# Five shifted sums packed without a gap, and two ScalarE copies of 400 elements in place of four of 200

## What is computed

```python
x = x + _L0_conv_ref(_gn(x), ...)   # sign, grouped 3x3 convolutions, batch norms
x = x + _L1_conv_ref(_gn(x), ...)   # deformable 3x3 attention over 8 groups
```

```python
off = om[..., :2 * K].reshape(n, h, w, G, K, 2) * OFFSET_SCALE
mask = om[..., 2 * K:]
...
sampled = gather(y0i, x0i, (1 - ty) * (1 - tx)) + gather(y0i, x0i + 1, (1 - ty) * tx) \
    + gather(y0i + 1, x0i, ty * (1 - tx)) + gather(y0i + 1, x0i + 1, ty * tx)
out = jnp.einsum('nhwgk,nhwgkc->nhwgc', mask, sampled)
out = out.reshape(n, L, c) @ op_w.T
```

## Time and profile before

| what | value |
| --- | --- |
| median of three runs | 2926.51 us |
| the profiled execution | 2924.83 us |
| its span, from the first instruction to the last | 2923.0 us |
| busy: TensorE, ScalarE, VectorE, GpSimd | 2430.8, 2259.7, 2205.6, 1917.6 us |
| `windows`, one pass (L1258) | 310 ns, x4032 |
| `copy_weights`, one copy (L1135) | 605 ns, x896 |
| `copy_om` (L960) | 1063 ns, x224 |

### The profile page before, as it was taken

The page is one execution under the profiler, slowest core; times in us unless marked ns, Lnnn a source line. Parts: engine busy times, 40 slices in busy tenths (PEclk is TensorE's granted clock), DMA queues, the critical chain, the costliest instruction groups (busy, mean ns, idle before and its releaser), DMA issues. The chain is left out here.

```text
span 2923.0 us, 100581 instructions
## 1 busy us (share of the span) xinstructions
PE 2430.8 (83%) x40456; PEld 2021.2 (69%) x40456; DVE 2205.6 (75%) x3095; ACT 2259.7 (77%) x4721; POOL 1917.6 (66%) x1452
## 2 busy tenths in 40 slices
PE   3999779993688888888888888888888888888887
PEld 2666556772577777777777777777777777777786
DVE  3555423334989897989888898989898988989773
ACT  2444256662989889898989898898989898989892
POOL 1000000003888888888988888888988898988892
PEclk8999889996899999999999999999999999999998
DMA  4555579975577677777777777777778777877675
GB/s 103 130 132 144 143 182 265 263 199 172 124 191 203 181 195 192 188 191 190 204 194 192 187 200 195 197 183 193 199 189 198 188 196 187 206 179 190 177 176 147
DMA packets 356164, 538.18 MB, mean 184 GB/s; under 512 B 171728, under 2 KB 258256, under 8 KB 355536
## 3 DMA queue, kind: packets, MB, share of 16 engines
q1 hardware_dynamic: 296656, 422.71, 60.3%
q10 hardware_dynamic: 59136, 110.11, 10.8%
HBM read 312.82 MB, written 219.77 MB: 182 GB/s over the span
## 5 line engine op out<-in xcount | busy, mean ns | idle before, releaser
L1109 ACT ACTIVATE dwt<-xp,wts 128x224 f32<-128x224 f32 x2016 | 797.3, 484 | 40.8 <-ACT wst L1135 31.8
L1280 PE MATMUL acc_p<-abuf,vbd 128*32 128x136 f32 (+5 forms) x20480 | 710.4, 291 | 54.9 <-issue 46.0
L1280 PEld LDWEIGHTS acc_p<-abuf,vbd 128*32 128x32 f32 (+1 forms) x20480 | 645.9, 145 | 117.7 <-issue 60.5
L979 DVE TENSOR_TENSOR pr<-mh_p,ht 128x864 f32<-128x864 f32 x672 | 668.9, 1051 | 23.2
L1258 PE MATMUL win_p<-pr,smat 128*128 128x160 f32 x4032 | 626.7, 310 | 27.3 <-POOL pr L1065 15.8
L246 PE MATMUL cv<-cin,wb 128*64 128x392 bf16 x6912 | 590.4, 333 | 25.8 <-ACT cin L225 25.8
L1258 PEld LDWEIGHTS win_p<-pr,smat 128*128 128x128 f32 x4032 | 570.4, 194 | 51.2 <-issue 22.4
L246 PEld LDWEIGHTS cv<-cin,wb 128*64 128x64 bf16 x6912 | 401.4, 110 | 208.7 <-ACT cin L225 25.9
L1048 POOL TENSOR_TENSOR dwt<-dwt 128x896 f32<-128x896 f32 x224 | 516.3, 2305 | 4.7 <-ACT dwt L1109 4.7
L1062 POOL TENSOR_TENSOR pr<-pr 128x576 f32<-128x576 f32 x224 | 317.3, 1417 | 187.8 <-DVE pr L979 187.8
L1135 ACT ACTIVATE wst<-win_p 128x200 f32<-128x200 f32 x896 | 388.6, 605 | 62.4 <-PE win_p L1258 38.7
(11 more groups left out here) (132 smaller groups left out, 2674.9 us busy)
## 6 DMA issues: line engine op xcount, KB each, us to landing
abuf<-weight_scratch SPq DMA_DIRECT2D x1568, 96.0 KB, 3.3
weight_scratch<-wst ACTq DMA_DIRECT2D x112, 960.0 KB, 6.2
xt<-x SPq DMA_DIRECT2D x128, 392.0 KB, 7.6
rows_scratch<-vsb SPq DMA_DIRECT2D x224, 128.0 KB, 2.1
vbd<-rows_scratch SPq DMA_DIRECT2D x896, 32.0 KB, 3.2
x_scratch<-xt SPq DMA_DIRECT2D x64, 392.0 KB, 6.6
y<-x SPq DMA_DIRECT2D x64, 392.0 KB, 4.4
x3h<-x_scratch SPq DMA_DIRECT2D x64, 392.0 KB, 4.9
```

Of the source, the lines that this page charges most:

```text
L979: dve.tensor_tensor(pr[:, j % 2, slots, :, :, :].rearrange("p k e x z -> p e k (x z)"), mh[:, a, :, :].rearrange("p (k x) z -> p k (x z)", ...
L1109: ins = act.activation(dwt[:, j % 2, k, :].rearrange("p (r w) -> p r w", w=W), image[:, r:r + BR, k % 3:k % 3 + W], ACT.Identity, scale=dw ...
L1280: mm = pe.matmul(acc_p[32 * (2 * s + b):32 * (2 * s + b) + 32, 0:2 * TN].rearrange("p (t w r) -> p t w r", t=BR, r=2)[:, t0:t1 + 1, x0:x1, :],
```

## The change

In PSUM, the five sums of `win_p` lay 172 columns apart, with gaps, in the order (shift, row, half b, pixel k, group). Now they follow each other at 160 columns, and within a row's 32 columns the order is group, then pixel. The order of the 32 is set where `oms` is made: `copy_om` now reads, for each of the 216 numbers of a row, the four rows' numbers, 256 elements apart in PSUM, and writes them side by side; before it read runs of four groups. `hats`, `mask_hats`, `products` and `merge` work element by element and are the same.

At 160 columns the fourth sum (e = 3) begins at column 480 and would cross the end of a PSUM bank at 512. So each of its two terms is computed in two matmuls, of 32 and of 128 columns.

`copy_weights` then needs two copies in place of four: for r = 0 and 1 it takes the two pixels of that parity. One copy goes over 4 groups x 50 (sums and half rows) x 2 pixels = 400 elements, and the cells of `wst` that it fills are the same as before. Before, neighbouring elements of a copy went to cells 480 elements apart (one group to the next); now pairs of them go to cells two elements apart.

```diff
-WP = 172
...
                     dve.tensor_tensor(
-                        oms[:, j % 2, :, :].rearrange("q w (b k g) -> q (w b) k g", b=2, g=GS),
-                        om_p[:, :].rearrange("q (k z) -> q k z", k=BR)[:, :, 0:OMC].rearrange("q k (v g) -> q v k g", g=GS),
-                        ombt[:, :].rearrange("q (v g) -> q v g", g=GS).unsqueeze(2).broadcast_to([LANES, 6 * TAPS, BR, GS]),
+                        oms[:, j % 2, :, :].rearrange("q w (g k) -> q (w g) k", k=BR),
+                        om_p[:, :].rearrange("q (k z) -> q z k", k=BR)[:, 0:OMC, :],
+                        ombt[:, :].unsqueeze(2).broadcast_to([LANES, OMC, BR]),
                         ALU.add).then_inc(om_ok, 1)
...
-                    for k in range(BR):
-                        to = 2 * BR * (2 - 2 * (k % 2)) + BR * u + k
+                    for r in range(2):
+                        to = 4 * BR * (1 - r) + BR * u + r
                         cells = wst[:, 0, to:to + 1]
                         ins = act.activation(
-                            bass.AP(cells.tensor, cells.offset, [cells.ap[0], [PC, CT], [2 * BR, 2 * RT], [BAND, GS]]),
-                            win_p[:, 0:CT * WP].rearrange("p (e z) -> p e z", e=CT)[:, :, 0:RT * BR * G].rearrange(
-                                "p e (m k g) -> p e m k g", k=BR, g=GS)[:, :, :, k, :],
+                            bass.AP(cells.tensor, cells.offset, [cells.ap[0], [PC, GS * CT], [2 * BR, 2 * RT], [2, 2]]),
+                            win_p[:, 0:CT * RT * BR * G].rearrange("p (m g k r) -> p r g m k", g=GS, k=2, r=2)[:, r],
                             ACT.Copy)
...
-                        to = WP * e
+                        cuts = (0, 1, RT) if e == 3 else (0, RT)
                         for n, (a, b) in enumerate(terms):
-                            mm = pe.matmul(win_p[:, to:to + 160], smat[:, e, :],
-                                           pr[:, j % 2, 0:RT, a, b, :],
-                                           start=n == 0, stop=n == len(terms) - 1)
+                            for m0, m1 in zip(cuts, cuts[1:]):
+                                mm = pe.matmul(win_p[:, BR * G * (RT * e + m0):BR * G * (RT * e + m1)], smat[:, e, :],
+                                               pr[:, j % 2, m0:m1, a, b, :],
+                                               start=n == 0, stop=n == len(terms) - 1)
```

## The result

The changed kernel takes 2937.93 us (median of 17 executions; the kernel before, in the same session, 2927.75, median of 18). An eighteenth execution of the changed kernel, slow at 4013.00 us with a granted clock of 0.557 where the others have 0.944 to 0.955, is left out. The ratio is 1.0034, 95% interval 1.0024 to 1.0044: slower by 0.34%, some 10 us, where the prediction said 4 us less. The time lies inside the stated range of 2905 to 2947 us, on the wrong side of the kernel before. The profiled execution took 2944.45 us (span 2942.7), 19.6 more than that of before, so the profile shows the effect somewhat too large.

What follows compares the result with a forecast made beforehand. With four engines nearly level, waits named the bound: GpSimd in some tiles, VectorE in those with next-image sums. Terms -5 + 3 - 2 + 0 = -4 us gave a 2922.5 us median; 8-in-10 range 2905 to 2947.

Steps and rivals of the forecast that it cites:

- What bounds the kernel: Loop over 224 tiles: four engines nearly level, so waits name the bound; hardly anybody waits for ScalarE.
- ScalarE's copies: Weight copies out of PSUM: 0.7 us less per tile, credited as -5 us, half of what others waited for ScalarE.
- TensorE's shifted sums (+3): The cut fourth sum's added matmuls: 0.3 us more per tile, mostly covered by waits, counted as +3 us.
- TensorE's clock (-2): Longer windows shorten TensorE's idle gaps before `misc`; a tenth fewer drops to half clock, -2 us.
- `oms` (0): VectorE's copy `oms`, now reading PSUM in steps of 1 KB: no longer than before, 0 us.
- The second: Rival: VectorE's `oms` pays for its strided PSUM read; 3024 us, or 2943 at half the price; chance 0.11.
- the fourth: Rival: ScalarE sets the pace after all, so all 157 us come back, 2770 us; chance 0.02.
- The third: Rival: TensorE becomes the bound between the sums, its work per tile passing GpSimd's 8.55 us; 2954 us; chance 0.07.
- The first: Rival: TensorE's and ScalarE's lateness is worth more: 8 us of half clock, 11 of waiting; 2910 us; chance 0.23.
- the signs for "wrong": `oms` above 1.4 us; VectorE's `misc` waits up over 20 us with TensorE's wait gone; or span falling with ScalarE's busy time.

Runs made afterwards that it cites:

- e1: Changed kernel with the sums starting at column 32, so no term is cut; new order and two copies stay: ratio to the kernel before 1.0032.
- e4: As e1 (new order, no cut), but with four copies of 200 elements in place of two of 400: ratio to the kernel before 1.0007.
- e2: Kernel before with only the two terms of the fourth sum cut into 32 and 128 columns, old layout and four copies: ratio to the kernel before 1.0033.
- e14: Changed kernel, with ScalarE waiting for its fourth tap to end before issuing the write of the weights: 2913.31 us, ratio to the kernel before 0.9962.
- e13: e1 with ScalarE waiting for its fourth tap to end before issuing the write of the weights: 2914.08 us, ratio to the kernel before 0.9960.
- e3: Kernel before with the fifth sum's term written twice by one matmul of 320 columns, longer passes without more instructions: ratio to the kernel before 0.9994.
- e9: e1 with the write of the weights placed behind the fifth of ScalarE's nine taps, without a wait: ratio to the kernel before 1.0028.

## Why the prediction was wrong, point by point

**What bounds the kernel** was read rightly as far as it went: VectorE waits for TensorE, GpSimd for VectorE, hardly anybody for ScalarE. What the reading left out were the rows "acc_p <- issue" and "win_p <- issue", 51 us, which were there in the trace of before.

**ScalarE's copies: the step that failed.** Their size was right, 1.68 us became 0.92 for the two (forecast 0.7 less; 530 ns each, a little over the 450 to 500 that were to be seen), and so was the end of the wait for `accs`, which has no row left in the changed kernel. The failing sentence is "Nothing moves on SyncE's or GpSimd's queues, the orders of the engines are the same [...] so its write stays one DMA". The write is on ScalarE's own queue, right behind the copies. It starts 1.2 us earlier against TensorE's `apply` (1.48 to 0.26), and there the packets of TensorE's instructions come only as it ends. In place of -5 us the copies brought +7 (e1 against e4). ScalarE's freed time went half into waiting for `oms` (85.6 us became 156.4) and half into waiting for `win_p` (25.4 became 98.6); the prediction had only the first. A step that gets shorter moves whatever it issues, and the prediction counted this for no queue but SyncE's and GpSimd's.

The Trainium skill, page "SBUF — State Buffer", section "Specifications (TRN2)", says that full bandwidth needs two hits per 16-byte line. The rows agree: 400 elements in pairs take 530 ns, 200 elements that jump 1,920 bytes 606 ns, and in e4 200 elements 32 bytes apart 582 ns. The -5 that hung on it did not come.

**TensorE's shifted sums (+3).** The length was right: 22 passes, 3.06 us against 2.71, +0.35 where 0.3 was taken. The price depends on what stands beside it: +11 us alone (e2), 1 us beside the two copies (10.2 us for after, 9.4 for e1, within their intervals), nothing beside the later write (e14 against e13). So in the kernel as it stood the term was sized more than three times too low, for a reason that is open; only beside the later write does the working, half of the few tiles without cover, come near what was measured.

**TensorE's clock (-2)** went the other way. Longer passes do lift it (e3: 0.956 over its runs, before 0.951), as argued, and in e3 they are free. But long halts inside `apply` and `windows` are followed by half clock as the gap before `misc` is the earlier trace rows: 12 of the 14 halts of over 2 us in the changed kernel are. Between 800 and 2800 us the traces have 46 stretches of half clock after, 35 before. The prediction knew one source of gaps only.

**`oms` (0)** was right: 1065 ns, and e4 costs nothing.

**The rivals.** The second (`oms`) and the fourth (ScalarE sets the pace) are out. The third had the sign and, at 2954, not the reason: in tiles without halts GpSimd still sets the pace (8.55 us from `mg1` to `mg1` in tiles 10 and 11 of e14, by its records). The first, 2910, is what the change gives when the write is moved out of the way, 2913, but the match is in part luck. Its larger term, 11 us of waiting for ScalarE, can have come (`misc` waited 0.7 us for `accs` in e14); its 8 us from a third fewer half-clock stretches did not, for e14 has 31 of them, before 35. Of the signs for "wrong" one came in part: VectorE's waits for `misc` grew by 28 us, but TensorE's wait before its next values fell from 181.8 to 130.5 us and was not gone.

## What to carry to other kernels

When a step gets shorter, follow every DMA that it issues to its new time, and ask what else uses the DMA engines just then, fetches of instructions included. In a long unrolled program look for "issue" waits inside a series of matmuls: here each ended 1.2 to 1.9 us after a packet of instructions had landed, and a large write that started just before made them longer. Don't count on compute instructions to delay a DMA that stands behind them on the same engine: on ScalarE in e9 they didn't, and a wait in e13 did.

## What the runs showed of the hardware that was not expected

- While the 960 KB write was on, no packet of q8 started (511 packets of the write in 3.7 us), though in e14 one starts within the first us of the same `apply`. The Trainium skill, page "DMA: Bandwidth & Descriptors", section "Queues, rings and completion order", says that each DMA engine takes turns between queues a packet at a time, and that a packet is typically 9 to 17 descriptors and at most 64. Spread evenly over 16 DMA engines the write's 512 records of 1,920 bytes are 32 for each (an estimate). By that rule, if a record is a descriptor, the instructions could get their turn in the middle of the write or only at its end. The trace doesn't decide between these: it shows when the packet came, at the end, and not when it was asked for.
- A halt of 3.37 us inside `apply` was followed by a granted clock of 0.50, and the `windows` behind it took 2.5 us more (5.56 against 3.06 us).
- A DMA that stands behind five taps on ScalarE (e9) left 0.03 us after the wait ahead of it was over, with four of the taps still to run.
